# Graph attention gather: ScalarE signals every weighed slot, GpSimd fetches the second row set slot by slot

## The chip, the cores and the metric

One core of one Trainium2 chip. The metric is the device time of one execution in microseconds, the median over runs. The engines are TensorE (PE in the profile), VectorE (DVE), ScalarE (ACT), GpSimd (POOL) and SyncE (SP).

## What is computed

A graph layer of 3125 nodes with 256 features. It adds to x an edge-wise attention (103125 edges, sorted by their target node; 4 heads of 64), a second-order linear attention over all nodes, and then a mixture of eight experts. The change lies in the edge-wise attention:

```python
q = (feat @ Wq).reshape(N, H, D)
k = (feat_c @ Wk).reshape(N, H, D)
v = (feat_c @ Wv).reshape(N, H, D)
e = jnp.einsum('ehd,ehd->eh', k[src], q[dst]) / jnp.sqrt(jnp.float32(H * D))
emax = jax.ops.segment_max(e, dst, num_segments=N)
ex = jnp.exp(e - emax[dst])
denom = jax.ops.segment_sum(ex, dst, num_segments=N)
a = ex / denom[dst]
m = v[src] * a[..., None]
ft2 = jax.ops.segment_sum(m, dst, num_segments=N).reshape(N, F)
```

## The kernel before, in words

`build` runs five stages one after the other: `stage_project` (k, v and q tables in HBM), `stage_edges_and_mix`, `stage_merge`, `stage_graph_ffn` and `stage_experts`. The change is in `stage_edges_and_mix`, which works through the edges in 113 tiles and does the second-order attention between their steps.

A tile has two row sets (G = 2), g = 0 and g = 1. A set has 128 rows, one to each partition, and each row has four slots (L = 4), one edge to a slot. So a tile needs eight fetches: one fetch is an indirect DMA in which GpSimd gathers, for one slot of 128 rows, 128 lines of the table `kv_tab`, 2 KB each (256 values of k and 256 of v). They land in a buffer `ring` of four tiles (RING = 4); tile n uses place n % 4.

What each engine does with tile n, one step of the loop to a tile; a step is cut in four quarters c = 0 to 3, and in each quarter PE, ACT and DVE also do micro-steps of the second-order attention, on which their order is written out by hand:

- **GpSimd** (L819 to L827): waits for the indices of the tile, then for set 0 until DVE has weighed set 0 of tile n - 4 (`val_ready`), issues four fetches; for set 1 until ACT has weighed all of set 1 of tile n - 4 (`act_val_ready`), issues four more. `pool.sem_inc(carrier, 1)` stands between the wait and the fetches, to carry the wait.
- **PE**: finds rows and nodes of tile n + 4 (L1260, L1266, L1267), takes each row's q out of a window of `q_tab` (L1275), and does the matmuls of the second-order attention, of which one or more stand in every quarter (L1308 for k, L1381 for q, read by ACT in L1193 and L1203, and the transposes read by ACT in L697).
- **DVE**: `times_q` multiplies the fetched k of each set with q, in place (L884, twice a tile, set 0 first; this is the first reader of the fetched rows, and waits for their landing); `add_up` sums by head (L889), then masks and maxima. In the next step `weigh` multiplies v of set 0 with its weights (L913, raises `val_ready`), and in quarter 3 `fold` (L921) adds slots 2 and 3 to slots 0 and 1, for both sets, and so waits for L913 and for ACT's four slots; `fold_on` (L927) adds the last two.
- **ACT**: `exps` (L1150, L1152) in quarter 3 makes the weights of tile n; `weigh_slot(n, e)` (L1160, four ACTIVATEs, one a head) weighs v of set 1, slot e: slot 0 in quarter 3 of step n, slots 1, 2 and 3 in quarters 0, 1 and 2 of step n + 1. Ahead of each stands the ACTIVATE of the quarter's micro-step, which needs PE. `settle_rows` (L1134, L1136) writes the indices of tile n + 4 after slot 2, `settle_nodes` (L1142, L1144) stands ahead of slot 3.
- **SP** loads the windows of q and the blocks of the edge table; the ACT queue stores the folded tile.

Of the kernel before, what the change touches and what calls it, by code (L numbers as in the profile page):

```python
# [53 lines left out]
L = 4  # L54
# [12 lines left out]
RING = 4  # L67
# [66 lines left out]
def wait(eng, sem, value):  # L134

    if not isinstance(value, int) or value > 0:
        eng.wait_ge(sem, value)
# [587 lines left out]
def stage_edges_and_mix(nc, a, t):  # L725
    x = t.mix
    with Memory(nc) as s:
# [19 lines left out]
        def spare(parts, *shape):  # L747
# [52 lines left out]
        scored, top_ready, less_ready, exp_ready, val_ready, act_val_ready, folded, folding, carrier = (  # L800
            s.sem("e_" + n) for n in ("scored", "top", "less", "exp", "val", "act_val", "folded", "folding", "carrier"))
# [15 lines left out]
        @block.gpsimd  # L817
        def _(pool):
            for n in range(TILES):  # L819
                pool.wait_ge(idx_ready, n + 1)  # L820
                for g in range(G):
                    wait(pool, (val_ready, act_val_ready)[g], n - RING + 1)
                    pool.sem_inc(carrier, 1)
                    for e in range(L):
                        pool.indirect_dma_start(out=ring[:, n % RING, g * L + e, :], out_offset=None, in_=t.kv_tab,  # L825
                                                in_offset=bass.IndirectOffsetOnAxis(ap=idx[n % 6][:, g, e:e + 1], axis=0)
                                                ).then_inc(landed[n % RING * 2 + g], 16)  # L827
# [36 lines left out]
        def _(dve):  # L864
# [52 lines left out]
            def fold(n):  # L917
                v = val[n % 2][:, :, :, :, :].rearrange("p g s h d -> p g (s h d)")
                dve.wait_ge(val_ready, n + 1)
                dve.wait_ge(act_val_ready, n + 1)  # L920
                dve.tensor_tensor(v[:, :, 0:2 * FD], v[:, :, 0:2 * FD], v[:, :, 2 * FD:], ALU.add).then_inc(folding, 1)  # L921

            def fold_on(n):
# [166 lines left out]
            for n in range(TILES + 1):  # L1090
# [29 lines left out]
                if old:  # L1120
                    fold(n - 1)
# [6 lines left out]
        def _(act):  # L1128
# [26 lines left out]
            def weigh_slot(n, e):  # L1155

                act.wait_ge(exp_ready, n + 1)
                act.wait_ge(landed[n % RING * 2 + 1], 16 * L * (n // RING + 1))
                for h in range(HG):
                    one = act.activation(val[n % 2][:, 1, e, h, 0:DG], ring[:, n % RING, L + e, F + h * DG:F + (h + 1) * DG], ACT.Copy,  # L1160
                                         scale=val[n % 2][:, 1, e, h, DG:])
                if e == L - 1:
                    one.then_inc(act_val_ready, 1)

            def keep_part(n):
                act.wait_ge(folded, n + 1)
# [63 lines left out]
            for n in range(TILES + 2):  # L1230
                for c in range(4):
                    *whole, last = micros(n, c)
                    for i in whole:
                        mix_first(i)
                        mix_last(i)
                    mix_first(last)
                    if c == 2 and n + AHEAD < TILES:
                        settle_nodes(n + AHEAD)
                    if c == 0 and n > 1:
                        keep_part(n - 2)  # L1240
                    if c == 3 and n < TILES:
                        exps(n)
                    mix_last(last)
                    if c == 3 and n < TILES:
                        weigh_slot(n, 0)
                    elif c < 3 and 0 < n <= TILES:
                        weigh_slot(n - 1, 1 + c)
                    if c == 1 and n + AHEAD < TILES:
                        settle_rows(n + AHEAD)
# [1195 lines left out]
```

## Time and profile before

| | us |
|---|---|
| median of 3 runs | 2665.03 |
| lowest and highest run | 2663.69, 2670.76 |
| profiled execution, its own time | 2674.8 |
| its span, first to last instruction | 2673.1 |

Mean granted TensorE clock of the span: 0.845. The profile is one execution. Busy time is of instructions on an engine; waits, branches and the issue of DMAs by SP and ACT are not counted, while a fetch by GpSimd (DMA_INDIRECT) is. A row of the waits says which instruction stood still, whose event ended it, the total, how often and the longest. "issue" says that no event ended the idle time just before the start; "remote" says that an event did whose sender the profile could not match.

### The profile page before, as it was taken

The numbers are of one execution on the slowest core, as the hardware profiler recorded it, in microseconds if no ns is written. First come the engines' busy times: TensorE is split into PE (matmuls) and PEld (weight loads), VectorE is DVE, ScalarE is ACT, GpSimd is POOL, SyncE is SP. The second block draws the span as 40 slices with busy tenths as digits, with TensorE's granted clock in tenths as the row PEclk, the third lists the DMA queues.
The fourth block names the chain that finished last, engine by engine and source line by source line (L and its number), as shares of the span: only waits on it lengthen the run. The fifth ranks groups of instructions, "written<-read, shape, count | busy, mean of one in ns | idle before, by whom it ended". The sixth has DMA issues, their size and how long they took to land. (4 is left out here: it accounts for less than half of the span.)

```text
span 2673.1 us, 45626 instructions
## 1 busy us (share of the span) xinstructions
PE 2071.7 (78%) x12642; PEld 1468.3 (55%) x12642; DVE 1745.4 (65%) x3439; ACT 1496.3 (56%) x4918; POOL 1213.7 (45%) x1183
## 2 busy tenths in 40 slices
PE   7757767678767657777777777765989986999998
PEld 4323332223323245555555555544778875999997
DVE  7367676767667675566666656676989996444443
ACT  2256556566556535565665655665875544555554
POOL 0455555555565545455455545542840001444443
PEclk9878788888888857788777777786999997999999
DMA  7666566666665655566556556545950017322221
GB/s 214 207 193 187 171 182 181 188 182 183 190 191 169 188 152 170 173 177 182 171 174 187 168 166 189 175 148 174 312 161 23 31 34 258 69 33 35 33 35 22
DMA packets 227731, 406.06 MB, mean 152 GB/s; under 512 B 58972, under 2 KB 129809, under 8 KB 227521
## 3 DMA queue, kind: packets, MB, share of 16 engines
q0 software_dynamic: 83712, 250.84, 33.7%
q1 hardware_dynamic: 120852, 116.88, 14.7%
q10 hardware_dynamic: 22957, 35.95, 3.7%
q8 instruction: 81, 1.33, 0.2%
q14 instruction: 129, 1.06, 0.1%
HBM read 345.66 MB, written 58.83 MB: 151 GB/s over the span
## 5 line engine op out<-in xcount | busy, mean ns | idle before, releaser
L825 POOL DMA_INDIRECT ring<-kv_tab,idx x904 | 915.4, 1013 | 769.5 <-ACT val L1160 449.8
L1160 ACT ACTIVATE val<-ring,val 128x64 f32<-128x64 f32 x1808 | 475.5, 336 | 15.5 <-DVE part L927 5.9
L921 DVE TENSOR_TENSOR val<-val 128x1040 f32<-128x1040 f32 x113 | 140.4, 1242 | 294.4 <-ACT val L1160 284.8
L884 DVE TENSOR_TENSOR ring<-ring,tile_bank 128x1024 f32<-128x1024 f32 x226 | 273.9, 1212 | 27.5 <-ACT tile_bank L1150 23.4
L1275 PE MATMUL tile_bank<-q_win,spread 128*128 128x256 f32 x452 | 180.7, 487 | 114.5 <-DVE val L913 68.9
L889 DVE TENSOR_REDUCE score<-ring 128x16 f32<-128x1024 f32 x226 | 267.7, 1208 | 0.0
L1308 PE MATMUL bank_f<-pair,u_T 96*125 96x496 bf16 x200 | 94.3, 471 | 180.7 <-ACT u_T L697 55.0
L2226 POOL DMA_INDIRECT out<-e_yw,to_row x56 | 120.8, 2157 | 222.0 <-DVE e_yw L2253 205.6
L2302 PE MATMUL e_h<-e_xT,e_now 128*128 128x128 f32 x1792 | 211.8, 277 | 0.7 <-DVE e_now L2243 0.7
L2302 PEld LDWEIGHTS e_h<-e_xT,e_now 128*128 128x128 f32 x1792 | 207.0, 194 | 1.2 <-DVE e_now L2243 1.1
L1308 PEld LDWEIGHTS bank_f<-pair,u_T 96*125 96x125 bf16 x200 | 29.4, 147 | 322.6 <-issue 122.0
L2317 PE MATMUL e_yps<-e_now,e_hT 128*128 128x256 f32 x896 | 202.5, 379 | 0.0
L2211 POOL DMA_INDIRECT xr<-rows,from_row x56 | 57.5, 1028 | 288.8 <-issue 288.5
L2267 ACT ACTIVATE e_now<-e_w_all 128x2048 f32 x56 | 106.9, 1912 | 131.2 <-PE e_yps L2317 131.2
L2317 PEld LDWEIGHTS e_yps<-e_now,e_hT 128*128 128x128 f32 x896 | 166.0, 190 | 20.3
L1275 PEld LDWEIGHTS tile_bank<-q_win,spread 128*128 128x128 f32 x452 | 89.5, 231 | 141.1 <-issue 111.1
L2275 ACT ACTIVATE e_hT<-e_h,small 128x128 f32<-128x128 f32 x448 | 127.6, 368 | 45.4 <-PE e_h L2302 45.4
L1381 PE MATMUL bank_f<-u_T,pair 96*124 96x125 bf16 x800 | 100.4, 259 | 62.2 <-ACT xn_buf L1187 49.2
L2251 DVE TENSOR_TENSOR e_y<-e_yps,small 128x256 f32<-128x256 f32 x56 | 23.8, 425 | 188.7 <-PE e_yps L2317 185.3
L1600 POOL TENSOR_TENSOR scaled<-g_ring,m_weights 128x325 f32<-128x325 f32 x137 | 106.8, 792 | 84.6 <-ACT m_weights L1582 60.6
L1203 ACT ACTIVATE phi<-bank_f 124x500 f32<-124x500 f32 x100 | 57.8, 578 | 148.9 <-PE bank_f L1381 75.1
L913 DVE TENSOR_TENSOR val<-ring,tile_bank 128x1024 f32<-128x1024 f32 x113 | 137.0, 1213 | 0.0
(423 smaller groups left out, 4956.3 us busy)
## 6 DMA issues: line engine op xcount, KB each, us to landing
g_ring<-parts SPq DMA_DIRECT2D x137, 260.0 KB, 4.3
parts<-part ACTq DMA_DIRECT2D x113, 260.0 KB
q_win<-q_tab SPq DMA_DIRECT2D x226, 128.0 KB
e_w_all<-L_ffn_W SPq DMA_DIRECT2D x16, 1024.0 KB, 11.7
ring<-kv_tab,idx POOLq DMA_INDIRECT x904
kv_tab<-kv_t SPq DMA_DIRECT2D x25, 224.0 KB
blocks<-t SPq DMA_DIRECT2D x216, 5.0 KB
blocks<-t SPq DMA_DIRECT2D x216, 0.0 KB
```

The costliest lines, as they stand in the source:

```text
L825: pool.indirect_dma_start(out=ring[:, n % RING, g * L + e, :], out_offset=None, in_=t.kv_tab, in_offset=bass.IndirectOffsetOnAxis(ap=idx[n ...
L884: dve.tensor_tensor(k, k, bcast(q_ps[g].unsqueeze(1), 128, L, F), ALU.mult).then_inc(q_read[g], 1)
L889: dve.tensor_reduce(score[:, :, g, :], ring[:, n % RING, g * L:(g + 1) * L, 0:F].rearrange("p s (h d) -> p s h d", h=HG), AX.X, ALU.add).t ...
L913: dve.tensor_tensor(val[n % 2][:, 0, :, :, 0:DG], ring[:, n % RING, 0:L, F:2 * F].rearrange("p s (h d) -> p s h d", h=HG), bcast(w_ps.unsq ...
L921: dve.tensor_tensor(v[:, :, 0:2 * FD], v[:, :, 0:2 * FD], v[:, :, 2 * FD:], ALU.add).then_inc(folding, 1)
L1160: one = act.activation(val[n % 2][:, 1, e, h, 0:DG], ring[:, n % RING, L + e, F + h * DG:F + (h + 1) * DG], ACT.Copy, scale=val[n % 2][:, ...
L1275: pe.matmul(q_ps[g], spread[n % NBUF][:, g, :], q_win[n % 2][:, g, :], start=True, stop=True).then_inc(q_ready[g], 1)
L1308: pe.matmul(kf_ps, k_.turned_parts[u % 2][:, k, 0:TP], x.pair3[:, :], start=True, stop=True).then_inc(kf_ready, 1)
L2226: pool.indirect_dma_start(out=out, out_offset=bass.IndirectOffsetOnAxis(ap=to_row[:, n:n + 1], axis=0), in_=yw[n % 2][:, :], in_offset=Non ...
L2275: gelu = act.activation(hT[j % 2][:, b, :], h_ps[j % 2][:, b, :], ACT.Gelu, bias=small[j][:, b:b + 1])
L2302: mm = pe.matmul(h_ps[j % 2][:, b, :], now1[j % 2][:, k, b * 128:(b + 1) * 128], xT[j % 2][:, k, :], start=(k == 0), stop=(k == FC - 1))
L2317: mm = pe.matmul(y_ps[j % 2][:, 0:F], hT[j % 2][:, b, :], now2[j % 2][:, b, :], start=(b == 0), stop=(b == HB - 1))
```

## The change

ACT raises `act_val_ready` after every slot instead of after slot 3 alone, so it counts to 4 a tile. DVE's `fold` waits for four times as high a count. GpSimd's single wait ahead of the four fetches of set 1 becomes one wait and one carrier increment ahead of each fetch, for that slot's count; the first four tiles have none. Set 0 stays as it was. Nothing else differs: the same fetches in the same order, the same sums.

```diff
                 for g in range(G):
-                    wait(pool, (val_ready, act_val_ready)[g], n - RING + 1)
-                    pool.sem_inc(carrier, 1)
+                    if g == 0:
+                        wait(pool, val_ready, n - RING + 1)
+                        pool.sem_inc(carrier, 1)
                     for e in range(L):
+                        if g == 1 and n >= RING:
+                            pool.wait_ge(act_val_ready, (n - RING) * L + e + 1)
+                            pool.sem_inc(carrier, 1)
                         pool.indirect_dma_start(out=ring[:, n % RING, g * L + e, :], out_offset=None, in_=t.kv_tab,
...
                 dve.wait_ge(val_ready, n + 1)
-                dve.wait_ge(act_val_ready, n + 1)
+                dve.wait_ge(act_val_ready, (n + 1) * L)
...
                     one = act.activation(val[n % 2][:, 1, e, h, 0:DG], ring[:, n % RING, L + e, F + h * DG:F + (h + 1) * DG], ACT.Copy,
                                          scale=val[n % 2][:, 1, e, h, DG:])
-                if e == L - 1:
-                    one.then_inc(act_val_ready, 1)
+                one.then_inc(act_val_ready, 1)
```

## Rows read from the trace of the kernel before

**Rows 1.** Busy time by stretch, the whole gather stage: engines, clock, DMA share, GB/s.
```profile
core 0: us, PE busy (x) PEld busy (x) DVE busy (x) ACT busy (x) POOL busy (x), PEclk, DMA share, GB/s
150.00:1790.00 1640.00, 1196.22 (x7383) 713.45 (x7383) 1098.66 (x1813) 962.93 (x3352) 885.09 (x872) 0.80 0.61 179
```

**Rows 2.** DMA queues, the gathers' own: packets, MB, share of 16 engines.
```profile
q0 software_dynamic: 83712, 250.84, 33.7%
```

**Rows 3.** Waits from 200 to 1700 us: total, times, longest, in us.
```profile
POOL ring L825 <- ACT val L1160: 429.1, 78, 12.5
DVE val L921 <- ACT val L1160: 261.3, 75, 7.2
...
ACT u_T L697 <- remote: 49.2, 7, 12.3
...
DVE ring L884 <- ACT tile_bank L1150: 19.4, 5, 7.9
```

**Rows 4.** Busy time by stretch, L825 alone, then L884 alone, to count.
```profile
0.00:1576.00 1576.00, 805.67 (x796) 0.80 0.62 182
...
0.00:1620.00 1620.00, 241.22 (x199) 0.80 0.62 181
```

**Rows 5.** Timeline of POOL, one burst: start, us, instruction, idle before it.
```profile
1565.80 1.38 POOL L825 DMA_INDIRECT ring<-kv_tab,idx  x1 [4.62 <-ACT val L1160]
...
1569.99 0.95 POOL L825 DMA_INDIRECT ring<-kv_tab,idx  x1 [0.30 <-issue]
1571.24 0.95 POOL L825 DMA_INDIRECT ring<-kv_tab,idx  x1 [0.30 <-issue]
...
1574.99 0.95 POOL L825 DMA_INDIRECT ring<-kv_tab,idx  x1 [0.30 <-issue]
```

**Rows 6.** Timeline of ACT around that burst, then of DVE.
```profile
1556.45 1.05 ACT L1160 ACTIVATE val<-ring,val 128x64 f32<-128x64 f32 x4
1557.40 0.15 ACT L1134 ACTIVATE idx<-tile_bank 128x8 int32<-128x8 f32 x1
...
1563.97 1.05 ACT L1160 ACTIVATE val<-ring,val 128x64 f32<-128x64 f32 x4
1564.92 0.56 ACT L1203 ACTIVATE xn_buf<-bank_f 124x500 f32<-124x500 f32 x1
...
1568.65 1.05 ACT L1160 ACTIVATE val<-ring,val 128x64 f32<-128x64 f32 x4
1577.50 1.00 ACT L697 ACTIVATE u_T<-bank_t 96x1000 bf16<-96x1000 bf16 x1 [7.79 <-remote]
...
1578.91 1.06 ACT L1160 ACTIVATE val<-ring,val 128x64 f32<-128x64 f32 x4
...
1583.46 1.05 ACT L1160 ACTIVATE val<-ring,val 128x64 f32<-128x64 f32 x4
...
1568.36 1.21 DVE L913 TENSOR_TENSOR val<-ring,tile_bank 128x1024 f32<-128x1024 f32 x1
...
1604.37 1.21 DVE L884 TENSOR_TENSOR ring<-ring,tile_bank 128x1024 f32<-128x1024 f32 x1
1618.33 1.21 DVE L884 TENSOR_TENSOR ring<-ring,tile_bank 128x1024 f32<-128x1024 f32 x1
```

**Rows 7.** Busy time by stretch, slices of 2 us in and after the burst; columns as rows 1.
```profile
1570.00:1572.00 2.00, 2.00 (x30) 1.51 (x28) 2.00 (x3) 0.00 (x0) 1.70 (x2) 1.00 0.73 261
1572.00:1574.00 2.00, 0.13 (x3) 0.00 (x0) 2.00 (x6) 0.00 (x0) 1.39 (x3) 1.00 1.04 391
1574.00:1576.00 2.00, 0.00 (x0) 0.00 (x0) 0.37 (x3) 0.00 (x0) 1.63 (x2) 1.00 0.76 213
...
1578.00:1580.00 2.00, 0.92 (x5) 0.92 (x6) 0.00 (x0) 2.00 (x9) 0.00 (x0) 0.50 0.01 2
```

## The prediction

> **What bounds the kernel now.** The view by stretch comes first. The stage that gathers edges fills 150 to 1790 us, 61% of the span, and the edit is in it alone. It issues 872 fetches there, 109 tiles of eight, so a tile takes 1640 / 109 = 15.0 us; of this PE is busy 11.0, DVE 10.1, ACT 8.8 and POOL 8.1 us [rows 1]. No engine is full, so the tile is set by waits. The gathers carry 250.84 MB, most of what the core moves [rows 2].
>
> Next, the waits. GpSimd (POOL) waits 429.1 us in 78 waits for ACT's last weighed slot (L1160), and this is what the edit loosens. DVE waits 261.3 us for the same slots before it folds (L921) [rows 3]. An idle GpSimd costs nothing unless somebody waits for what it fetches, so look there: the product that first reads fetched rows (L884) waited in all 19.4 us, in 5 waits, for an ACT exponential, and no row names a landing. How early the rows are there can be counted. Up to 1576 us there are 796 fetches, 99 tiles and the first row set of tile 99; the last of them is issued at 1574.99 and done at 1575.94, and the product on it, the 199th L884, starts at 1618.33 [rows 4 to 6]. That is 42.4 us after the issue ends, nearly three tiles. **Read alone, this says that earlier fetches are worth nothing.**
>
> But the stretch around one burst of fetches shows something else. Burst: eight fetches, 1565.80 to 1575.94, first the second row set of a tile (released by slot 3, weighed by 1565.02), then, with no pause, the first row set of the next (1571.24) [rows 5, 6]. Two-us slices: from 1572 to 1574 PE is busy 0.13 us, from 1574 to 1576 nothing of PE or ACT runs and DVE only 0.37 us, while DMA moves 391 and 213 GB/s. From 1578 to 1580, with 2 GB/s, ACT is busy all the time again [rows 7]. ACT's row says the same: L697 starts at 1577.50 after 7.79 us, released by "remote", here a PE completion seen long after its matmul's recorded end, since only one core runs [rows 6]. In the stage L697 alone stands so 49.2 us, 7 times [rows 3]. So some 6.2 us into a burst (1572.0 - 1565.8) the loop stops, and goes on some 1.6 us after its last fetch ends (1577.50 - 1575.94): a stop of 5.5 us. **What the fetches cost is their bunching, and the edit changes the bunching.** That is an inference from the trace; it is the step on which the forecast stands.
>
> The Trainium skill, page "SBUF — State Buffer", section on the two physically separate sides (engine ports and AXI ports), says that engine accesses and DMA do not contend. The slices do not show which resource is short, but they show idle engines beside heavy DMA. By the page the burst would not matter, and the sum below would be 0; that is the first rival.
>
> **The change, part by part.**
>
> *ACT's increment on each slot:* three more per tile, 339 in all. Four L1160 and what follows start 0.95 us apart in slot 2, which has no increment now (1556.45 to 1557.40), and 0.95 us in slot 3, which has one (1563.97 to 1564.92) [rows 6]. Cost 0, and behind it only the next ACTIVATE.
>
> *DVE's wait before the fold:* (n + 1) x 4 is reached by the same instruction as n + 1 was. Cost 0.
>
> *GpSimd's waits:* one wait and one carrier increment for the second set become four of each, from tile 4 on. One that is already met shows no cost: the fetch at 1571.24 stands behind an index wait, a DVE wait and an increment, and starts 0.30 us after its forerunner like those behind no wait [rows 5]. One that really waits costs 0.78 us from the slot's end (1563.97 + 1.05 = 1565.02) to the fetch at 1565.80, and that fetch takes 1.38 instead of 0.95 us: 1.21 us in all [rows 5, 6]. Queued behind such a wait are the tile's later slots and the next tile's first set, and their readers are covered by the 42 us above (33 us for a second set, whose last fetch goes at 1569.99 and which is read at 1604.37 [rows 5, 6]). DMA bytes and count are the same; SP's and ACT's own DMAs keep their order. Were the cover gone, each real wait would cost its 1.21 us.
>
> *When the fetches go.* Before: slot 3 of tile m opens four, DVE's weighing (L913) opens four more, in time to make eight in a row. After: L913 opens the first four; slots 0 and 1 are weighed by then (slot 1 ends at 1569.70, L913 at 1569.57), slot 2 and slot 3 may not be. In the cycle shown they are weighed at 1579.97 and 1584.51, 10.4 and 14.9 us after L913 [rows 6], while four fetches and slots 0 to 2 take only 7 x 1.25 = 8.75 us. With these times the burst breaks after six or seven fetches and the traffic drains before the last. But the times are not fixed: that the slots are late is the stop's doing, which will fall elsewhere (the burst starts at 1570.3 instead of 1565.8, 4.5 us later in the loop). Unstopped, slot 3 would come within the first 6 us and all eight would still run together.
>
> **The size.** A burst shorter by one fetch shortens the stop by 1.25 us. Of a stop of 5.5 us, DVE feels what it waits for slots, 261.3 us over the window's 1500 / 15.0 = 100 tiles, 2.6 us a tile or 0.47 of it; the rest is covered by its own work. I take it that half the tiles break their burst: between none (slots ready) and all (times as in the cycle shown), with nothing to weigh one end over the other. Gain: 109 x 1.25 x 0.47 x 0.5 = 32 us. Bounds: at the one end all of DVE's 261.3 us go, since no wait for slots would be left; at the other the real waits lengthen every burst by 1.21 us and with it every stop: 109 x 1.21 x 0.47 = 62 us lost.
>
> Sum against the profiled execution: 2674.8 us (span 2673.1 and 1.7 around it) less 32 is 2643. It lies 10 us above the median of the runs, 2665.03; on the median's scale the forecast is 2633 us.
>
> **The rivals.**
> 1. *Nothing moves* (within 0.3%, about what a measurement of this kernel can tell from no change): 2665 us. For it: the 42 us of cover, no landing among the waits, and the page's rule. Or the stop is real but follows the burst: later in the loop, as long, with all eight fetches again in a row. Against it: 0.3% is 8 us, or 0.07 us a tile, and a burst 4.5 us later against the loop should move more than that one way or the other.
> 2. *Slower, by a longer burst.* Place: GpSimd, at slot 2 or 3. If the slot comes less than about 1.6 us after the fetch before it, the traffic does not drain and the stop does not lift, yet the real wait is paid: 1.21 us longer burst and stop, 0.47 felt, +62 us, 2727. It decides if real waits show on the last slots with pauses of only one or two us. The same price holds if the first set's gate (L913) opens under the stop, so that the next four fetches follow on at once: with 12 in a row a stop grows by 5.0 us, and one such tile in four costs as much as rival 2 does. For: DVE ran on for 2 us of this stop. Against: such chains are then cut at slot 2, which ACT reaches only with PE.
> 3. *Much faster*: the two gates and four slots spread the fetches so that no burst passes 6 us; the stop goes, DVE's wait goes with it, down to 2665 - 261 = 2404. POOL's 8 x 1.25 = 10.0 us in a tile of 15.0 leave room, but a spread that even needs all slots late, which the vanished stop would cure. I give it little.
> 4. *It doesn't do what it says*: all slots are weighed when GpSimd gets there. Then only the start is moved; this is rival 1.
>
> **How the numbers follow.** Forecast (somewhat faster, one or two tiles in three with a broken burst, 2601 to 2657) 0.40; much faster 0.05; nothing 0.23; slower 0.32. Range: the bounds of the forecast's own case (all tiles broken: -64, to 2601) and of rival 2 (+62, a little inside since not every tile would pay); 2595 to 2720 leaves out the 0.05 below, most of it, and the tails above. Faster and slower both hold much; the forecast's own range is 2601 to 2657.
>
> **What would show it.** In the profile after: L825's waits split over L913 and single L1160 releases; L825's busy time up by 0.43 us for each real wait; fetch bursts of six or seven beside single fetches, not eights. "Remote" waits of ACT and DVE's wait at L921 (261.3 us) fall by a tenth or more. L884 still waits for no landing. L1160 keeps its 0.95 us. PE's granted clock should stay near 0.80 in the stage [rows 1]. Wrong: if bursts break and the "remote" waits don't shrink, bunching is not the cause of the stop; if bursts stay at eight and the time moves, it is the place of the burst in the loop; if L884 waits for landings, the cover was misjudged.

## The result: slower by 3.4%

| | before | after |
|---|---|---|
| median of 4 runs each, us | 2666.61 | 2757.86 |
| lowest and highest, us | 2663.69, 2670.76 | 2744.26, 2770.12 |
| profiled execution: its time, span | 2674.8, 2673.1 | 2744.26, 2742.5 |

Ratio 1.034, 95% interval 1.029 to 1.039. The forecast (2633 us, range 2595 to 2720) was wrong, in sign and in range. The medians differ by 91 us, the two profiled executions by 69 to 71 us: the one before lies 8 us above its median, the one after is the fastest of its four.

The whole loss lies in the gather stage. From the first L913 to the last, the kernel before takes 1654.9 us and the changed one 1725.6. That is 70.7 us more, and the two spans differ by 69.4: nothing outside the stage counts. Busy time by stretch, after, same stretch as [rows 1]:

```profile
core 0: us, PE busy (x) PEld busy (x) DVE busy (x) ACT busy (x) POOL busy (x), PEclk, DMA share, GB/s
150.00:1790.00 1640.00, 1172.85 (x6907) 680.35 (x6907) 1058.82 (x1747) 922.17 (x3203) 848.38 (x840) 0.78 0.59 172
```

840 fetches instead of 872 in the same 1640 us, 15.6 us a tile instead of 15.0; every engine does less in the stretch. The waits after, as [rows 3] (total, times, longest, in us, 200 to 1700 us; L829 was L825, L1164 was L1160, L925 was L921, L888 was L884):

```profile
POOL ring L829 <- issue: 500.9, 691, 8.3
POOL ring L829 <- ACT val L1164: 214.4, 78, 6.3
DVE val L925 <- ACT val L1164: 157.3, 44, 8.5
...
DVE val L925 <- issue: 90.4, 38, 6.4
...
ACT u_T L697 <- remote: 41.7, 13, 7.5
...
DVE ring L888 <- ACT tile_bank L1154: 37.1, 16, 6.0
```

GpSimd's wait for ACT's slots is halved, as the change intends, but its idle time as a whole is not less. Its row by "issue", which holds the 0.30 us between two fetches and real waits whose event the profile did not match, was

```profile
POOL ring L825 <- issue: 261.2, 720, 7.5
```

before and is 500.9 us now: 429.1 + 261.2 = 690.3 us before, 214.4 + 500.9 = 715.3 after. The wait has moved from ACT's slot to DVE's weighing. DVE's wait before the fold is hardly shorter: 157.3 + 90.4 = 247.7 us against 261.3 + 6.1 = 267.4 (the 6.1 us are the "issue" row of L921 before), and in fewer tiles, 96 instead of 100. Its wait for the exponentials has doubled (19.4 to 37.1), and no row names a landing. All "remote" rows of ACT and DVE together: 451.9 before, 500.1 after. One cycle, on GpSimd (timeline: start, us, instruction, idle before it):

```profile
1518.02 0.94 POOL L829 DMA_INDIRECT ring<-kv_tab,idx  x1 [5.25 <-issue]
1519.27 0.94 POOL L829 DMA_INDIRECT ring<-kv_tab,idx  x1 [0.30 <-issue]
...
1525.55 0.94 POOL L829 DMA_INDIRECT ring<-kv_tab,idx  x1 [0.30 <-issue]
1529.27 1.37 POOL L829 DMA_INDIRECT ring<-kv_tab,idx  x1 [2.77 <-ACT val L1164]
1533.59 0.94 POOL L829 DMA_INDIRECT ring<-kv_tab,idx  x1 [2.95 <-issue]
```

and on ACT and DVE:

```profile
1522.95 0.59 ACT L1206 ACTIVATE phi<-bank_f 124x500 f32<-124x500 f32 x1 [3.01 <-issue]
1526.51 0.47 ACT L1146 ACTIVATE spread<-tile_bank,pcol 128x256 f32<-128x256 f32 x1 [2.97 <-remote]
...
1527.43 1.05 ACT L1164 ACTIVATE val<-ring,val 128x64 f32<-128x64 f32 x4
...
1516.03 1.22 DVE L917 TENSOR_TENSOR val<-ring,tile_bank 128x1024 f32<-128x1024 f32 x1
...
1518.96 2.34 DVE L893 TENSOR_REDUCE score<-ring 128x16 f32<-128x1024 f32 x2
...
1522.30 0.18 DVE L912 TENSOR_TENSOR less<-own,m_all 128x32 f32<-128x32 f32 x1
1528.58 1.24 DVE L925 TENSOR_TENSOR val<-val 128x1040 f32<-128x1040 f32 x1 [6.10 <-ACT val L1164]
```

The burst starts when L917 (L913 before) ends, 1517.25, runs for seven fetches to 1526.49, breaks, and slot 3's fetch goes alone at 1529.27, 0.79 us after ACT weighed the slot at 1528.48. The bursts broke as forecast: counting fetches less than 0.7 us apart as one burst, before has 59 bursts of eight, 19 of four and 10 of twelve among 111; after has 77 single fetches, 40 sevens and 30 eights among 170. Of the 77, 57 are the last slot of a tile, so 57 of the 109 tiles that are gated break there. The start moved as well. In the changed kernel at least nine in ten of the bursts of four or more begin 0.8 us after the end of L917; before, half of them begin later than 11.1 us after L913, in a tile of 14.9. The stop did not go. Here DVE ends its sums and the small work on them at 1522.48 and then stands 6.10 us, till ACT, late by PE, has weighed slot 3. In the burst of [rows 5 to 7] DVE was busy until 1574.4, 8.6 us after the burst began; here it stands 4.5 us after its start (1518.02 to 1522.48). What the stop costs in one cycle varies, though: DVE stood even longer there, 9.22 us, so the comparison rests on the sums by tile further down.

```profile
1574.20 0.17 DVE L651 TENSOR_SCALAR u_nrm<-u_nrm 125x8 f32<-125x8 f32 x1
1583.59 0.42 DVE L1018 TENSOR_TENSOR xn_buf<-bank_o,y_inv 128x250 f32<-128x250 f32 x1 [9.22 <-ACT y_inv L1215]
```

### The profile page after: what moved, and what is told of

Read it like the earlier page. It is cut to its first block and busy times, and to the rows that moved or that the text cites. A ratio compares the mean times of both kernels' runs of the same rounds, so it can differ in the third digit from the quotient of the medians.

```text
span 2742.5 us, 45949 instructions
## 1 busy us (share of the span) xinstructions
PE 2105.3 (77%) x12642; PEld 1478.6 (54%) x12642; DVE 1749.4 (64%) x3439; ACT 1500.4 (55%) x4918; POOL 1209.5 (44%) x1183
## 3 DMA queue, kind: packets, MB, share of 16 engines
q0 software_dynamic: 83712, 250.84, 33.5%
## 5 line engine op out<-in xcount | busy, mean ns | idle before, releaser
L829 POOL DMA_INDIRECT ring<-kv_tab,idx x904 | 912.6, 1010 | 837.5 <-issue 598.0
L1164 ACT ACTIVATE val<-ring,val 128x64 f32<-128x64 f32 x1808 | 477.1, 339 | 12.8 <-DVE part L931 8.5
L925 DVE TENSOR_TENSOR val<-val 128x1040 f32<-128x1040 f32 x113 | 140.5, 1243 | 289.2 <-ACT val L1164 173.7
L888 DVE TENSOR_TENSOR ring<-ring,tile_bank 128x1024 f32<-128x1024 f32 x226 | 274.5, 1215 | 49.0 <-ACT tile_bank L1154 48.8
L1384 PEld LDWEIGHTS bank_f<-u_T,pair 96*124 96x124 bf16 x800 | 79.8, 169 | 112.5 <-issue 68.8
```

What stands on the lines that cost most here:

```text
L888: dve.tensor_tensor(k, k, bcast(q_ps[g].unsqueeze(1), 128, L, F), ALU.mult).then_inc(q_read[g], 1)
L1384: mm = pe.matmul(qf_ps[k % 2][:, b, :], x.pair3[:, b * PB:(b + 1) * PB], q_.turned_parts[u % 2][:, k, 0:TP], start=True, stop=True)
```

## Experiments

Eighteen results follow, in the order in which they ran; each set shares one chip and its own runs of the kernel before, and the ratio is to those. The kernel before took 2697, 2677, 2676 and 2704 us in four of the six sets, and 2289 and 2290 us in the other two, which ran on one and the same chip. That difference between chips is itself a finding, told below.

**full_count.** Only the count waited for differs from the changed kernel.

```diff
-                            pool.wait_ge(act_val_ready, (n - RING) * L + e + 1)
+                            pool.wait_ge(act_val_ready, (n - RING) * L + L)
```

> The changed kernel, but each of the four waits of GpSimd ahead of set 1 asks for the full count of the old tile, (n - 4) x 4 + 4, so the fetches go as in the kernel before, with all the new increments and waits in place. If the signals themselves cost (ACT's 339 increments, GpSimd's waits and carriers): near the changed kernel, some 2750 us. If only the order in time of the fetches costs: 2667 us, as before, and bursts of eight again.

2695.76 us, ratio 1.0003 (0.997 to 1.004). The increments, and waits that are already met, are free, as the prediction had it; the price is in when the fetches go. (A wait that is real, one slot after another, is not in this run.)

**dve_gates.** From the kernel before:

```diff
-                    wait(pool, (val_ready, act_val_ready)[g], n - RING + 1)
+                    wait(pool, val_ready, n - RING + 1 + g)
```

> The kernel before with set 1 of tile n released by DVE's weighing of tile n - 3 instead of by ACT's slots, set 0 as it was. Then GpSimd has one gate a tile, L913, and sends set 1 and the next set 0 as one burst of eight from L913 on. If the place of the burst in the loop costs (it starts at L913 in the changed kernel and after slot 3 in the one before): slow, 2720 to 2760 us, with bursts of eight. If the broken burst and its real waits cost (rival 2 of the prediction): about 2667 us, since no slot is waited for.

2846.01 us, 1.0545 (1.052 to 1.057): slower than the change itself, with 81 bursts of eight among 97 and no wait for a slot. Unbroken bursts cost more when they start at L913. Waits, 200 to 1700 us:

```profile
POOL ring L825 <- DVE val L913: 590.1, 75, 14.8
...
DVE val L921 <- ACT val L1160: 226.0, 51, 10.6
...
ACT spread L1142 <- remote: 88.4, 26, 11.6
DVE slv_acc L964 <- remote: 81.3, 13, 9.4
```

All its "remote" rows sum to 585.7 us, 134 more than before.

**act_gate.** One wait for slot 3 (and the L913 that stands ahead of it) before set 0, none before set 1.

```diff
-                    wait(pool, (val_ready, act_val_ready)[g], n - RING + 1)
-                    pool.sem_inc(carrier, 1)
+                    if g == 0:
+                        wait(pool, act_val_ready, n - RING + 1)
+                        wait(pool, val_ready, n - RING + 1)
+                        pool.sem_inc(carrier, 1)
```

> The kernel before with the old tile's slot 3 asked for ahead of set 0, not only of set 1: one gate a tile, slot 3, and then set 0 and set 1 of one tile as one burst of eight. It starts where the burst of the kernel before starts. Place of the burst: about 2667 us or a little less, since the second gate no longer breaks a burst. Broken bursts: the same. If it is clearly slower than before, neither holds.

2745.77 us, 1.0194 (1.017 to 1.022). Its bursts start where those before do (median 11.7 us after the end of L913, against 11.1), and yet it is slower, so by its own expectation neither theory holds as it stands. It fetches both sets of one tile together, and 72 of its 103 bursts are eights and none are fours; which of this costs the 1.9% is open. It is still 3.5% below dve_gates, which also has mostly bursts of eight.

**half_fetches.** `for e in range(L if n < RING else L // 2)`, with the counts of the landings to match.

> The kernel before with only slots 0 and 1 of each set fetched from tile 4 on; slots 2 and 3 are computed on whatever the buffer still holds. GpSimd has 4 fetches a tile instead of 8, all other instructions stay. If the fetches' traffic stops the loop (the step on which the forecast stood): the stage falls from 15 to 11 or 12 us a tile, so 300 us or more off the whole, and the remote waits nearly vanish. If the traffic has no part in it, as the landings are never waited for: within 10 us of 2667.

2337.01 us in one run, 360 us off; half the fetches are left out, so it computes something else and serves for its time alone. None of its waits of ACT or DVE, 200 to 1700 us, is "remote"; what is left is

```profile
POOL ring L825 <- ACT val L1160: 494.3, 105, 13.5
POOL ring L825 <- issue: 299.8, 314, 5.2
DVE val L921 <- ACT val L1160: 129.1, 84, 4.8
```

So, on this chip, the stops are the fetches' doing, and they take some 3.1 us of every tile (14.94 to 11.82).

**pairs, fours, half_bytes.** Pairs: a wait ahead of every second fetch, for L913, L889 (set 1), L921 and L884 (set 0) in turn, each raised by DVE after the old tile is done with. Fours: `(val_ready, folding)[g]` for the two sets. half_bytes: `out=ring[..., 0:F]` from the table seen as rows of 256.

> The kernel before with four gates a tile, each ahead of two fetches: DVE's weighing (L913), its second sum by head (L889), its fold (L921) and its first product with q (L884), a few us apart in DVE's order; eight fetches a tile as before. If the stop comes from bunching, it shrinks towards what half_fetches showed with the same groups of two: 2400 to 2600 us, remote waits below 100 us. If it comes from the amount of traffic alone: 2667 or worse by GpSimd's four real waits a tile, at 1.21 us each, up to 2750 us.

> The kernel before with set 1 released by DVE's fold (L921) instead of by ACT's slot 3: the same four and four, the second four some 2 us later than slot 3 alone. If bunching costs: two bursts of four where they don't touch, and a time between those of pairs and before, 2600 to 2680. If the place of the fetches in the loop costs: a shift of 1 to 2 us of the second four towards the next L913, so between before and dve_gates, 2680 to 2750 us.

> The kernel before, but from tile 4 on each fetch brings rows of 1 KB instead of 2 KB (the other half is computed on what the buffer holds, and the rows are others). GpSimd issues as many fetches of as many rows in the same places. If the stop comes from the bytes under way: near half_fetches, 2340 to 2420 us. If it comes from the number of fetches and their descriptors: near 2667 us.

2293.59 us, 1.0013 (0.999 to 1.004); 2290.81, 1.0016 (1.000 to 1.004); 2294.89. But here the kernel before took 2289.23 us. On this chip the traces of all three have no "remote" wait of ACT or DVE, though pairs has bursts of up to 252 fetches. So the same fetches stop the loop on one chip and not on another; the three tell nothing of the stops, and two were repeated.

**after_again, pairs_again, half_bytes_again.** The same kernels on a chip with stops.

> The changed kernel itself, beside the kernel before on one chip. The kernel before took 2666 and 2697 us on two chips and 2289 us on a third, where no trace shows a remote wait. If the change costs by when the fetches make the stop fall: slower by about 3.4% where the kernel before takes some 2670 us, and equal within 0.3% where it takes some 2290 us. If the change costs by itself (signals, real waits on the slots): slower on either chip.

2752.56 us, 1.031 (1.024 to 1.038), where before takes 2677.34: the result repeats.

> The four gates a tile once more, for a chip with stops. Bunching: clearly below the kernel before where that takes some 2670 us (2400 to 2600). Amount of traffic: 2667 or above. On a chip without stops: equal to before, as it was.

2722.45 us, 1.0179 (1.011 to 1.024). Four gates did not spread the fetches: under a stop the later gates were all met by the time GpSimd came to them, and 67 of its 128 bursts are still eights. So this run says nothing against bunching, which its expectation overlooked.

> Fetches of 1 KB rows once more, for a chip with stops. If bytes under way make the stop: no remote waits and a time near that of half_fetches (2337 us). If the number of fetches and their descriptors: near the kernel before on that chip.

2675.63 us, beside 2677.34, with 136.55 MB instead of 250.84 on the queue and the stops as they were:

```profile
q0 software_dynamic: 55808, 136.55, 19.3%
```

```profile
POOL ring L825 <- issue: 270.4, 717, 9.6
DVE val L922 <- ACT val L1161: 245.3, 77, 7.9
ACT phi L1204 <- remote: 78.7, 18, 7.7
```

Bytes are not it (one run).

**gate_sum, gate_fold, gate_product.** One gate for all eight fetches of a tile, at three more places of DVE's order. The diff is gate_sum's; gate_fold waits for `folding, n - RING + 1` and gate_product for `q_read[0], n - RING + 3`.

```diff
+                    if g == 0 and n >= RING:
+                        pool.wait_ge(reduced[1], n - RING + 3)
+                        pool.sem_inc(carrier, 1)
```

> The kernel before with one gate a tile for all eight fetches: DVE's second sum by head (L889) of tile n - 2, some 5 us after its weighing (L913). Place theory: the burst starts about where slot 3 is weighed when nothing stops, so near act_gate, 1.00 to 1.03 times before. If any single gate of DVE costs what dve_gates cost: 1.055. On a chip where before takes some 2290 us: equal.

> One gate a tile for all eight fetches: DVE's fold (L921) of tile n - 4, some 2 us later than gate_sum and 2 to 3 us ahead of the next L913. Place theory: the stop then starts 2 to 3 us after L913 and falls on DVE's sums, which need no PE: 0.98 to 1.02 times before, the cheapest place or near it. Single DVE gate: 1.055. On a chip without stops: equal.

> One gate a tile for all eight fetches: DVE's first product with q (L884, set 0) of tile n - 2, 1.2 us ahead of L913 of the same step. Place theory: near dve_gates, which starts 1.2 us later: 1.03 to 1.055 times before. If the place has no part in it, it equals gate_fold and gate_sum. On a chip without stops: equal.

1.0288 (1.020 to 1.037), 1.0396 (1.033 to 1.046), 1.0444 (1.038 to 1.051). In the order of DVE's loop, from one L913 to the next, the single gates give 1.0545 (L913), 1.029 (sum), 1.019 (slot 3), 1.040 (fold), 1.044 (product), 1.0545 (the next L913); in the traces the median burst of four or more starts 0.8, 4.8, 11.7 and 13.7 us after the end of L913 for the first four. The place counts: cheapest is about slot 3, dearest is L913. But gate_fold was expected to be the cheapest and is not: my picture of what the stop falls on was wrong there. The sum of the "remote" rows does not measure the loss either: gate_sum has 444.9 us of them, less than the 451.9 before, and is 2.9% slower.

**direct_loads.** half_fetches, and SyncE loads the missing slots with plain DMAs of fixed rows.

> half_fetches with the missing slots 2 and 3 of each set loaded by SyncE instead, as plain DMAs of 128 rows of 2 KB from a fixed place of the same table, so as many bytes land as in the kernel before; the rows are not those of the edges. If any DMA traffic of this size stops the loop: near the kernel before. If it is GpSimd's gathers: near half_fetches, 2337 us where before takes 2690.

2340.26 us, beside 2675.92, and no "remote" wait. The same bytes land in the same buffer, and nothing stops. Together with half_bytes_again this clears the DMA traffic. The slices of [rows 7] showed idle engines beside 391 GB/s, and I read a cause into it. The Trainium skill, page "SBUF — State Buffer", section "SBUF: two separate sides" (engine and AXI ports), has engines and DMA not contending; by these two runs the traffic is not what stops them, which agrees.

**half_rows, pause_4, pause_2.** half_rows: `rows = slice(0, 128 if n < RING else 64)` on output and index. pause_4 and pause_2: a fill on GpSimd, of bytes that nobody reads, after every fourth or second fetch. The diff is pause_2's.

```diff
+                        if e % 2 == 1:
+                            wait(pool, idled, (n * G + g) * (L // 2) + e // 2)
+                            pool.memset(idle, 0).then_inc(idled, 1)
```

> The kernel before, but from tile 4 on each fetch brings 64 of its 128 rows; the other 64 are computed on what the buffer holds. As many fetches, half as many rows and bytes. If each fetch as such holds the loop: near the kernel before. If the rows, with GpSimd's work on each, do: towards half_fetches, 2340 to 2500 us, with fewer remote waits. On a chip where before takes some 2290 us it tells nothing.

2713.75 us, beside 2703.84: rows are not it either (one run). What is left is the gather instruction itself, or the time that GpSimd is in it: a fetch of 64 rows still takes 0.91 us, so these two are not told apart.

> The kernel before with a fill of 1200 bytes on GpSimd after every four fetches (some 1.3 us, nobody reads it). If a pause of 1.5 us lifts the stop, as the end of a burst does: remote waits fall, the tile nears the 13.5 us that GpSimd then needs, 2500 to 2640 us. If the pause is too short or the number of fetches counts: GpSimd is busy longer and it gets slower, 2700 to 2900 us. On a chip without stops: 200 us slower or so than before, as GpSimd becomes the bound there.

2496.94 us, 0.925 (0.921 to 0.930): **faster than both kernels.** The fill takes 1.12 us.

> A fill of 800 bytes (some 0.9 us) after every two fetches. If pauses lift the stop even when short: like pause_4 or better in remote waits, with a tile of 14 us by GpSimd. If they don't: slower than pause_4.

2448.64 us, one run, 0.906 of 2703.84. GpSimd in it:

```profile
1550.98 0.78 POOL L832 MEMSET xn_buf<- 128x800 uint8 x1
1551.92 0.95 POOL L827 DMA_INDIRECT ring<-kv_tab,idx  x1 [0.16 <-issue]
1553.18 0.95 POOL L827 DMA_INDIRECT ring<-kv_tab,idx  x1 [0.30 <-issue]
1554.13 0.78 POOL L832 MEMSET xn_buf<- 128x800 uint8 x1
```

and the waits, where 62.0 us of DVE's 261.3 are left and 21 us of "remote" in all:

```profile
POOL ring L827 <- issue: 196.8, 843, 0.3
...
DVE ring L889 <- DMA ring<-kv_tab,idx: 168.4, 74, 3.8
...
DVE val L926 <- ACT val L1165: 62.0, 46, 5.5
...
ACT xn_buf L1208 <- remote: 8.0, 11, 1.6
```

As many fetches of as many bytes; GpSimd never waits, and is now late: for the first time DVE waits for landings before its product (L889 was L884), 168.4 us in 74 waits, and 73.5 in pause_4. Yet the loop hardly stops any more. All that differs is the fill of 0.8 us after each pair; whether it is the break in the run or the lower rate of fetches inside it that helps is not told apart. The rate over a whole tile is not it, since it rose: eight fetches in 13.0 us instead of 14.9.

**after_pause_2.** The changed kernel with the fills of pause_2.

> The changed kernel with the same fill of 800 bytes after every two fetches as pause_2. If the change costs only by where the stops fall: no stops, nothing to lose, 0.90 to 0.92 times before as pause_2 was (0.906). If the real waits on the slots cost by themselves: up to 1.21 us a tile, 5% more than pause_2, 0.95 or above.

It ran on a chip without stops: 2453.63 us, where before takes 2290.43, 1.071 (1.068 to 1.075). So the pauses, with the change, cost 7% there, and GpSimd is the bound with them: four times 3.15 us (from one fill to the next, 1550.98 to 1554.13 in pause_2) is 12.6 of pause_2's 13.0 a tile, and DVE waits 199.5 us for landings. Beside pause_2, which took 2448.64 us on a chip with stops, the changed kernel is within 0.2%: with GpSimd never early for a slot, slot by slot seems to cost nothing. That is an indication only, since it compares two chips and pause_2 has a single run, and since there are then no real waits on slots to pay for. What the change does without pauses on a chip without stops was not timed.

## Why the change is slower

First, what a stop is. In the cycle of [rows 6] ACT's L697 starts at 1577.50 and waits for these matmuls, whose record ends at 1570.44:

```profile
1569.84 0.60 PE L691 MATMUL bank_t<-identb,u_parts 125*96 125x125 bf16 x8
```

The trace has their semaphore event at 1577.47, 7.03 us after that end. Over the 108 tiles of the table below, an event of PE comes 0.015 us (median) after the last recorded end of a matmul that raises its semaphore. But over 2 us late are 54 of 260 before (up to 13.5 us), 60 of 268 after, 31 of 224 in pause_4, 9 of 224 in pause_2 (none over 2.8 us), none in half_fetches, and none of 309 in pairs on the chip without stops. A few matmul records are missing in a trace, so single counts can be somewhat off.

The clock goes with it. After the stop of [rows 7] PE runs at a granted 0.50 (1.2 GHz), having been busy 0.13 us of the 4 us to 1576. Busy time by stretch, columns as [rows 1], for before, after, dve_gates and pairs:

```profile
200.00:1400.00 1200.00, 864.24 (x4681) 478.98 (x4682) 808.35 (x1350) 699.10 (x2433) 649.50 (x640) 0.80 0.61 178
200.00:1400.00 1200.00, 853.12 (x4405) 457.52 (x4407) 792.05 (x1321) 678.48 (x2364) 631.29 (x625) 0.78 0.60 174
200.00:1400.00 1200.00, 818.41 (x3948) 425.39 (x3946) 744.50 (x1246) 636.12 (x2207) 574.14 (x588) 0.76 0.56 163
200.00:1400.00 1200.00, 999.44 (x7092) 610.38 (x7094) 1024.76 (x1700) 901.13 (x3136) 843.33 (x833) 0.88 0.77 232
```

With the granted clock, PE's busy time a tile goes from 9.7 us in pairs to 10.9 before, 11.2 after and 11.5 in dve_gates. So a part of what the stops cost is the lower clock behind them; no run takes it alone.

Reading each profiled trace in steps of 0.05 us, from the third L913 to the 111th (108 tiles), gives per tile how long GpSimd is in fetches (0.4 us before each start included, and a step that is touched counted whole), and how much of DVE's, ACT's and PE's work is done outside that time, in us:

| kernel (all with stops) | tile | in fetches | DVE outside | ACT outside | PE outside |
|---|---|---|---|---|---|
| before | 14.94 | 10.61 | 1.09 | 3.03 | 2.93 |
| full_count | 15.00 | 10.63 | 0.97 | 3.09 | 2.91 |
| act_gate | 15.52 | 10.64 | 1.24 | 3.46 | 3.42 |
| after | 15.57 | 10.66 | 2.95 | 3.49 | 3.32 |
| gate_sum | 15.86 | 10.56 | 3.82 | 3.51 | 4.00 |
| gate_fold | 15.93 | 10.41 | 2.34 | 4.03 | 4.04 |
| gate_product | 16.14 | 10.37 | 3.30 | 4.18 | 4.09 |
| dve_gates | 16.57 | 10.36 | 3.83 | 4.39 | 4.40 |
| pause_4 | 13.64 | 10.96 | 1.60 | 1.74 | 2.05 |
| pause_2 | 12.98 | 11.02 | 1.60 | 1.28 | 1.49 |

Wherever the fetches go, GpSimd spends some 10.5 us of a tile in them, and a tile is that time and the rest. The rest grows with the work that is left for it: from before to dve_gates it grows by 1.9 us and the tile by 1.6, with ACT's work outside the fetches up 1.4 and PE's 1.5. Down the eight kernels without pauses ACT's column never falls as the tile grows, and PE's hardly does; DVE's does not follow the tile (3.82 in gate_sum at 15.86, 2.34 in gate_fold at 15.93). A burst that starts at slot 3 is followed by fold, products, weighing and sums, 9 of DVE's 10 us, which run on while PE's completions are late. A burst that starts at L913 finds 3.6 us of it, then the fold, which needs ACT's late slots. The change moves the start of the burst to L913 and loses 0.63 us a tile in the profiled executions, 70 us in 110 tiles (by the medians 91 us, 0.8 a tile). That it is not as slow as dve_gates I put down to the fetch that is held back to its slot (in 57 of 109 tiles); no run takes that alone.

Shown is that the place of the burst changes the time, from 1.9% (slot 3) to 5.5% (L913) among the single gates. Argued and not shown is why one place is dearer than another. The order of DVE's work does not settle it: by that argument gate_fold was to be the cheapest, and dve_gates and gate_sum leave the same DVE work outside the fetches (3.83 and 3.82 us) with tiles of 16.57 and 15.86. ACT's and PE's work fits better, but it is a correlation.

## The prediction, point by point

- *The stage and its waits, landings never waited for:* right, for before and after. Only the kernels with pauses wait for landings.
- *Signals and DVE's count cost 0:* right (full_count 1.0003). L1160, four at a time, takes 1.05 us before and after.
- *A burst of fetches stops the loop:* right on this kind of chip, and shown by half_fetches and the pauses. That DMA's traffic does it, which the slices suggested, was wrong.
- *Bursts would break:* right, and in 57 of 109 tiles; "half the tiles" was right.
- **The step that failed:** "A burst shorter by one fetch shortens the stop by 1.25 us", and with it the 32 us of gain. The fetch taken out of the burst is not gone; it falls into the stretch that had been free. Time in fetches a tile stayed 10.61 to 10.66 us, and the free stretch grew from 4.3 to 4.9. The shift of the whole burst by 4.5 us, which the prediction named in passing ("the stop's doing, which will fall elsewhere") and priced at nothing, was the term that decided; dve_gates has it without a wait for any slot and costs 147 us (1.0545). What the broken burst gives back by itself stays open: no run has it without the shift.
- *Rival 2, slower by 62 us:* right in sign, but by luck, and it is 91 us by the medians. Its mechanism, real waits making each burst and stop 1.21 us longer, was not what happened: full_count and the time in fetches show no longer burst, and dve_gates, without any wait for a slot, is slower still.
- *What would show it:* "if bursts break and the remote waits don't shrink, bunching is not the cause" was written down. They broke and didn't shrink, and bunching is the cause nevertheless: a burst of seven is not broken enough. Pairs with 0.8 us between them are. DVE's wait at the fold was to fall by a tenth or more and fell by 7% (267.4 to 247.7 us), and PE's granted clock in the stage went from 0.80 to 0.78.

## What to carry to other kernels

An engine that is not waited for can still cost by what it does to the others while it works; look at what stands still during its runs, not only at who waits for its output. Before trusting a coincidence (idle engines beside heavy DMA), vary bytes, rows and instruction count one at a time. A run of GpSimd gathers longer than a few us is worth breaking with short idle work where the trace shows completions arriving late, and not elsewhere: time it on more than one chip.

## Hardware behaviour that was not expected

- Unbroken indirect DMAs of GpSimd, one each 1.25 us, hold up PE's completions by up to 13.5 us on some chips. In the kernel before, steps of 0.1 us with a "remote" stand of ACT or DVE are some 4% of the first us of a burst, half at 8 to 10 us and three quarters at 15 to 20. It depends on the number of gathers (half as many: no "remote" row), not on rows (2713.75 us with half, beside 2703.84) or bytes (2675.63 beside 2677.34), and a fill of 0.8 us after each pair takes the "remote" rows from 451.9 to 21 us.
- The kernel before took 2666.6 to 2703.8 us in five sets of runs (the result's own among them) and 2289.2 and 2290.4 in two, both on one chip. The traces from that chip have no stops, even with a burst of 252 fetches. That the whole difference of 375 us or more is the price of the stops is not shown by itself, but half_fetches, which ends them on another chip, takes off 360 us. What differs between the chips is open, as is what in a gather holds PE's completions.
- A fetch by GpSimd takes 0.95 us for 128 rows and 0.91 for 64 (medians). What it waited for counts: after a real wait for ACT's slot it takes 1.38 us (median of 84 before), after one for DVE's L913 0.94 (median of 89 in dve_gates). Of the prediction's 1.21 us for a real wait, the 0.43 us of a longer fetch hold for the first kind alone.
